# A mixture-of-experts stage in units of 120 rows, two units of an expert per task, task list made on the chip

## What is computed

```
x = x + tanh(g0) * attention(layernorm(x), context)      # one 32-wide head, tiled, @ Wout + bout
z = layernorm(x)
probs = softmax(z @ router_w.T)                          # 8 experts
weights, indices = top_k(probs, 2); weights /= sum + 1e-6
gate, up = split(z @ w13[e])                             # 512 -> 2 x 1024
y[e] = (silu(gate) * up) @ w2[e]                         # 1024 -> 512
x = x + tanh(g1) * sum over the two chosen e of weights * y[e]
```

## Time and profile before

| | |
|---|---|
| median of 3 runs | 400.83 us (398.74 to 402.16) |
| the profiled execution | 402.54 us |
| its span, first to last instruction | 400.9 us |
| PE busy | 375.2 us, 94% |
| PEld, DVE, ACT, POOL busy | 285.9, 221.8, 190.7, 143.1 us |
| HBM read | 70.95 MB |

### The profile page before, as it was taken

One profiled execution on the slowest core, in us unless ns is written; L12 is line 12 of the kernel. 1 busy time (PEld: TensorE's weight loads), 2 busy tenths in 40 slices (PEclk: granted clock), 3 DMA queues, 4 the chain that ended last, 5 costly groups with the idle time before them and its releaser, 6 DMA issues.

```text
span 400.9 us, 7148 instructions
## 1 busy us (share of the span) xinstructions
PE 375.2 (94%) x2034; PEld 285.9 (71%) x2035; DVE 221.8 (55%) x448; ACT 190.7 (48%) x313; POOL 143.1 (36%) x245
## 2 busy tenths in 40 slices
PE   3979799987999999999989999999999999999993
PEld 3335355565788888887868888888888888888882
DVE  3341767876934951899731249518932962694120
ACT  1123256656625832888621258328723842682220
POOL 2630768777333222514233242132303322331301
PEclk9977699999699999999999999999999999999997
DMA  7997689932169992499961239915952792200211
GB/s 251 361 366 262 239 294 356 266 134 69 17 246 398 368 327 45 138 346 352 356 203 30 27 52 336 314 35 138 337 214 53 260 329 91 46 26 7 34 18 17
DMA packets 18793, 77.79 MB, mean 194 GB/s; under 512 B 4827, under 2 KB 6075, under 8 KB 11612
## 3 DMA queue, kind: packets, MB, share of 16 engines
q1 hardware_dynamic: 11836, 66.82, 46.4%
q0 software_dynamic: 5184, 7.54, 9.9%
q10 hardware_dynamic: 1760, 3.28, 2.5%
HBM read 70.95 MB, written 7.58 MB: 196 GB/s over the span
## 4 chain that ended last, share of the span: by engine, by line
PE 61%; DMA 19%; POOL 6%; issue 6%; POOLq 2%; DVE 2%; ACT 1%; SPq 0%; DVEq 0%
PE scp L500 15%; PE turnB L480 14%; PE turnA L480 14%; DMA out_dram<-yw,ent 7%; DMA ent_next<-lists_d 7%; PE kvp L316 5%; PE kvp L487 2%; DMA xn<-in_x_dram 2%; PE turnA L369 2%; POOL ent_next L1123 1%; PE turnA L354 1%; PE scp L467 1%; DMA xg<-xn_d,ent_next 1%; PE scp L342 1%; DMA lists_d<-entry,place 1%
## 5 line engine op out<-in xcount | busy, mean ns | idle before, releaser
L847 DVE TENSOR_TENSOR w13l<-stage,w13h 128x1024 fp32r<-128x1024 f32 x64 | 75.9, 1218 | 4.7 <-ACT w13h L610 4.7
L610 ACT ACTIVATE w13h<-stage 128x1024 fp32r<-128x1024 f32 x64 | 65.0, 1053 | 0.0
L480 PE MATMUL turnA<-w13h,xTh 128*128 128x512 f32 x128 | 51.7, 404 | 2.1 <-DVE xTl L973 2.1
L480 PE MATMUL turnB<-w13h,xTh 128*128 128x512 f32 x128 | 51.9, 405 | 0.0
L480 PE MATMUL turnA<-w13l,xTh 128*128 128x512 f32 x128 | 51.4, 401 | 0.0
L480 PE MATMUL turnA<-w13h,xTl 128*128 128x512 f32 x128 | 51.4, 401 | 0.0
L500 PE MATMUL scp<-w2h,hTh 128*128 128x512 f32 x128 | 51.3, 401 | 0.0
L480 PE MATMUL turnB<-w13l,xTh 128*128 128x512 f32 x128 | 50.5, 395 | 0.0
L480 PE MATMUL turnB<-w13h,xTl 128*128 128x512 f32 x128 | 50.5, 394 | 0.0
L500 PE MATMUL scp<-w2h,hTl 128*128 128x512 f32 x128 | 50.1, 391 | 0.0
L500 PE MATMUL scp<-w2l,hTh 128*128 128x512 f32 x128 | 50.1, 391 | 0.0
(11 more groups left out here) (179 smaller groups left out, 632.0 us busy)
## 6 DMA issues: line engine op xcount, KB each, us to landing
stage<-in_w_dram SPq DMA_DIRECT2D x48, 1024.0 KB, 5.4
ctx_t<-in_ctx_dram SPq DMA_DIRECT2D x8, 1444.0 KB, 12.8
xT_t<-in_xT_dram SPq DMA_DIRECT2D x8, 200.0 KB, 12.1
xn<-in_x_dram SPq DMA_DIRECT2D x8, 200.0 KB
xn_d<-xn ACTq DMA_DIRECT2D x8, 200.0 KB
stage<-in_wout_dram SPq DMA_DIRECT2D x1, 1024.0 KB, 13.8
out_dram<-x ACTq DMA_DIRECT2D x4, 200.0 KB
out_dram<-yw ACTq DMA_DIRECT2D x2, 200.0 KB
```

The lines of the kernel that those rows point to most:

```text
L480: mm = pe.matmul(region, xp[:, c, :], wp[:, q, c, :], start=(c == 0 and i == 0), stop=(c == HC - 1 and i == 2))
L610: act.activation(dst, src, ACT.Copy).then_inc(S["w_hi"], 1)
L847: dve.tensor_tensor(lo, raw, hi.bitcast(F32), ALU.subtract).then_inc(S["w_lo"], 1)
```

## The change

- **Units.** Rows are handled in units of U = 120. List capacity per expert grows to 840 rows. A task is either a *single* (one unit) or a *pair* (two units of one expert, 240 rows).
- **Task list.** Task 0 is the first unit of expert 0. Then come the pairs of all experts, in order, then the odd units of all experts, in order. DVE and PE compute the row and the expert of each task (`task_row`, `task_e`) and the ends of the loops (`bounds`). The two matmuls for the table stand in task 0, behind its gate/up 0; the reads of the table by DVE give `tiles_ready`, for which POOL (first list read), SP (first load of the next weights) and the loops wait. Before, `tile_row` was made ahead of the first tile.
- **Weights.** They are loaded and split once per task, not per expert: every task, task 0 and the last included, splits the weights of the next one. For the last this is a load that nobody uses.
- **Single.** As a tile before, with 120 rows; x of both units of the next task is transposed (8 transposes, the second four into kvp). Its splits stand where they stood in a tile with splits.
- **Pair.** Gate/up holds a 128 x 128 block of w13 as the stationary operand and streams the 240 rows of x past it: 8 rounds of 24 matmuls. The result has h's features on partitions, so h is not transposed. Down is as before, once for each unit.
- **Task 0.** The low parts of units 4 to 9 of expert 0's weights are made between its products (`first_single`).
- **Rows.** Two gathers, two weight gathers and two scatters per task; xg_b and yw_b are second buffers.

```diff
+    U = 120
+    U2 = 2 * U
+    CAP = (-(-T // U) + 1) * U
...
-            sp.wait_ge(S["gathered"], 16)
-            with sp.Fori(1, E) as e:
+            sp.wait_ge(S["gathered"], 32)
+            sp.wait_ge(S["tiles_ready"], 1)
+            loads_end = sp.value_load(bounds[0:1, 2:3], min_val=2, max_val=TILES - 1)
+            with sp.Fori(1, loads_end) as t:
+                e = sp.value_load(task_e[0:1, bass.ds(t, 1)], min_val=0, max_val=E - 1)
                 for q in range(NQ):
-                    sp.wait_ge(S["w_lo"], e * W_UNITS - W_UNITS + 2 * q + 2)
+                    sp.wait_ge(S["w_lo"], t * W_UNITS - W_UNITS + 2 * q + 2)
...
+            def make_table():
+                pe.wait_ge(S["tabs_made"], 10)
+                pe.matmul(scp[0:1, 64:64 + TILES], ones[0:E, 0:1], tabs[:, 5, :], start=True, stop=True)
+                pe.matmul(scp[0:1, 128:128 + TILES], e_col[:], tabs[:, 6, :], start=True, stop=True).then_inc(S["table_done"], 1)
...
+            def single(t, aside=None):
+                gate_up(t, 0)
+                if aside is not None:
+                    aside()
+                gate_up(t, 1)
+                gate_up(t, 2)
                 turn_h(t, 0)
                 turn_h(t, 1)
-                gate_up(t, 3, e)
-                down(t, 0, e)
+                gate_up(t, 3)
+                down(t, 0)
                 turn_h(t, 2)
                 turn_h(t, 3)
-                turn_x(t + 1)
...
+                turn_x(t + 1, 0)
+                down(t, 1)
+                pe.wait_ge(S["hl_done"], 8 * t + 14)
+                turn_x(t + 1, 1)
+                down(t, 2)
+                down(t, 3)
+
+            def gate_up_pair(t, r):
+                if r == 0:
+                    pe.wait_ge(S["xl_done"], 2 * t + 2)
+                pe.wait_ge(S["h_done"], 8 * t + r + 5)
+                q, j = r // 2, r % 2
+                bank = (turnA, turnB)[r // 2 % 2][:, j * 512:(j + 1) * 512]
+                terms = ((w13h, xTh), (w13h, xTl), (w13l, xTh))
+                for part in range(2):
+                    cols = slice(part * QW + j * P, part * QW + (j + 1) * P)
+                    for c in range(HC):
...
+                        for i, (wp, xp) in enumerate(terms):
+                            mm = pe.matmul(bank[:, part * U2:(part + 1) * U2], wp[:, q, c, cols], xp[:, c, :],
+                                           start=(c == 0 and i == 0), stop=(c == HC - 1 and i == 2))
+                mm.then_inc(S["gu_done"], 1)
...
+            def pair(t):
+                for r in range(2 * NQ):
+                    gate_up_pair(t, r)
+                down_pair(t, 0)
+                turn_x(t + 1, 0)
+                turn_x(t + 1, 1)
+                pe.sem_inc(S["ht_done"], 2 * NQ)
+                down_pair(t, 1)
+
+            pe.sem_inc(S["xg_turned"], 2)
+            single(0, make_table)
+            pairs_end, tasks_end = task_ends(pe)
+            with pe.Fori(1, pairs_end) as t:
+                pair(t)
+            with pe.Fori(pairs_end, tasks_end) as t:
+                single(t)
...
+            def single(t):
 
                 def split(*units):
-                    if e_next is not None:
-                        for unit in units:
-                            split_hi(e_next, unit, t)
+                    for unit in units:
+                        split_hi(t + 1, unit, t)
 
                 silu(t, 0)
                 split(0, 1)
...
+            def pair(t):
+                for r in range(2 * NQ):
+                    silu_pair(t, r)
+                    if r > 0:
+                        h_hi_pair(t, r - 1)
+                    if 0 < r < 2 * NQ - 1:
+                        split_hi(t + 1, r - 1, t)
...
+            def first_single():
+                split_lo(0, 4)
+                split_lo(0, 5)
+                h_mul(0, 0)
+                split_lo(0, 6)
+                split_lo(0, 7)
+                h_mul(0, 1)
+                split_lo(0, 8)
+                h_mul(0, 2)
+                h_lo(0, 0)
+                h_lo(0, 1)
+                split_lo(0, 9)
+                h_mul(0, 3)
+                h_lo(0, 2)
+                h_lo(0, 3)
+                split_lo(1, 0)
+                x_lo(1)
+                for unit in range(1, W_UNITS):
+                    split_lo(1, unit)
...
+            make_tabs()
             make_weights()
+            read_table()
             dve.wait_ge(S["lists_sent"], 1)
-            for unit in range(4, W_UNITS):
-                split_lo(0, unit)
...
+            first_single()
...
-            with pool.Fori(1, n_tiles) as t:
+            with pool.Fori(1, tasks_end) as t:
                 entries_stay(t)
                 read_list(row_of(t + 1))
-                hold(S["xg_turned"], t + 1)
+                hold(S["xg_turned"], 2 * t + 2)
                 gather(t + 1)
                 gather_weights()
-                add_rows(t - 1)
+                add_rows(t)
                 entries_pass(t)
                 pool.drain()
```

More of the change, by code:

```diff
@@ L219, in unit_of, with task_ends @@
             return down[:, u * IC // 2:(u + 1) * IC // 2, :]
[L221 to L230, removed]
+        def task_ends(eng):
+            eng.wait_ge(S["tiles_ready"], 1)
+            return (eng.value_load(bounds[0:1, n:n + 1], min_val=2, max_val=TILES - 1) for n in range(2))
         @block.sync
@@ new lines, in down_pair @@
+            def down_pair(t, u):
+                if u == 0:
+                    pe.wait_ge(S["y_ready"], 2 * t + 2)
+                pe.wait_ge(S["w_lo"], t * W_UNITS + 2 * NQ + 1 + u)
+                terms = ((hTh, w2h), (hTl, w2h), (hTh, w2l))
+                for k in range(2):
+                    for j in range(u * IC // 2, (u + 1) * IC // 2):
+                        if k == 0:
+                            pe.wait_ge(S["hl_done"], 8 * t + j + 9)
+                        for i, (hp, wp) in enumerate(terms):
+                            mm = pe.matmul((scp, kvp)[k][0:U, 512:512 + H], hp[:, j, k * U:(k + 1) * U], wp[:, j, :],
+                                           start=(j == 0 and i == 0), stop=(j == IC - 1 and i == 2))
+                    if u == 1:
+                        mm.then_inc(S["y_done"], 1)
+                if u == 0:
+                    mm.then_inc(S["y_half"], 1)
@@ L603, in split_hi @@
                     if unit < 2 * NQ:
-                        act.wait_ge(S["gu_done"], NQ * last + NQ + unit // 2 + 1)
+                        act.wait_ge(S["gu_done"], 8 * last + 2 * (unit // 2) + 2)
                     elif unit == 2 * NQ:
@@ L665, in _, with h_hi_pair @@
+            def h_hi_pair(t, r):
+                act.wait_ge(S["h_done"], 8 * t + r + 9)
+                act.wait_ge(S["y_done"], 2 * t + 2)
+                act.activation(hTh[:, r, :], h_t[:, r % NQ, 0:U2], ACT.Copy).then_inc(S["hh_done"], 1)
             first_x_hi()
@@ new lines, in read_table @@
+            def read_table():
+                dve.wait_ge(S["table_done"], 1)
+                dve.tensor_scalar(task_row[:], scp[0:1, 64:64 + TILES], float(E * CAP), None, ALU.add).then_inc(S["rows_read"], 1)
+                dve.tensor_copy(task_e[:], scp[0:1, 128:128 + TILES]).then_inc(S["rows_read"], 1)
+                dve.wait_ge(S["rows_read"], 2)
+                dve.sem_inc(S["tiles_ready"], 1)
+            def x_lo(t):
+                for k in range(2):
+                    dve.wait_ge(S["xh_done"], 2 * t + k + 1)
+                    cols = slice(k * U, (k + 1) * U)
+                    dve.tensor_tensor(xTl[:, :, cols], (scp, kvp)[k][:, 0:HC * U].rearrange("p (c s) -> p c s", c=HC),
+                                      xTh[:, :, cols].bitcast(F32), ALU.subtract).then_inc(S["xl_done"], 1)
@@ L951, in split, with single @@
+            def single(t):
                 def split(*units):
-                    if e_next is not None:
-                        for unit in units:
-                            split_lo(e_next, unit)
+                    for unit in units:
+                        split_lo(t + 1, unit)
                 h_mul(t, 0)
@@ new lines, in pair @@
+            def pair(t):
+                for r in range(2 * NQ):
+                    h_mul_pair(t, r)
+                    if r > 0:
+                        h_lo_pair(t, r - 1)
+                    if 0 < r < 2 * NQ - 1:
+                        split_lo(t + 1, r - 1)
+                h_lo_pair(t, 2 * NQ - 1)
+                for unit in range(2 * NQ - 2, 2 * NQ):
+                    split_lo(t + 1, unit)
+                x_lo(t + 1)
+                for unit in range(2 * NQ, W_UNITS):
+                    split_lo(t + 1, unit)
@@ L985, in _ @@
-            t0, t1 = tiles_of(dve, E - 1)
-            with dve.Fori(t0, t1) as t:
-                tile(t, None)
+            first_single()
+            pairs_end, tasks_end = task_ends(dve)
+            with dve.Fori(1, pairs_end) as t:
+                pair(t)
+            with dve.Fori(pairs_end, tasks_end) as t:
```

(1 more changed line is left out.)

341 lines of the change are left out of this document (194 added, 147 removed).

## The result

The changed kernel takes 413.1 us (411.97 to 415.0, 4 runs), the one before, in the same session, 401.0: a ratio of 1.030. Some executions of a kernel are over 1.5% slower than its fastest one; the ratios with intervals in this document leave those out on both sides, so they differ a little from the ratio of the medians: here 1.037, with a 95% interval of 1.032 to 1.042. It is slower. Forecast were 412.0 us, 398 to 425, and a ratio of 1.028. The profiled execution, 413.6 us with a span of 412.0, ends where the sum of the prediction ended (412.1).

What follows compares the result with a forecast made beforehand. TensorE, busy 94% of the span, was taken to bound the kernel. Pair 1's start at 141.5, 0.4, six pairs of 34.5, three singles of 18.8, then 6.8 and 1.6 gave 413.7 us, on the median 412.0; range 398 to 425.

Steps and rivals of the forecast that it cites:

- Task 0: First single: silu 1 waits behind a load, TensorE stands for 16 us, pair 1 begins at 141.5, 20 us later.
- the splits ahead of the pair's first product: Start of pair 1: DVE works through eight units first, TensorE has four banks in hand; at most 0.5 us.
- The pair: Two units on TensorE: 34.5 us against 36.0 for two tiles; six pairs save 9 us.
- the 0.118 us of a 240-column matmul: Pairs' gate/up: 100 ns of columns plus 16 to 20 ns; 192 matmuls make 22.7 us.
- The singles: Last three tasks: each 18.4 us plus 0.4 for four more transposes, 18.8; three are 56.4 instead of 54.
- its lead of a pair covers that: Singles: POOL's lead covers 4.5 us of added gathers and scatters over three tasks; without it up to 10 us, none taken.
- The rival of the late POOL: POOL and DMA engines bound the singles: 22 instead of 18.8 us, up to 4 more in the stall, 420 to 425; chance 0.13.
- The dummy load: Load of task 10 at the end: lies behind task 9's y_out or beside the last scatter, costs nothing.
- Cheaper narrow matmuls: Pairs' gate/up: a matmul costs 0.100 us, a pair 31.1, the kernel 391; chance 0.10.
- Loads that are not hidden: Pairs' gate/up: operand load not hidden behind a narrow matmul, 0.211 us each, + 107 us, 519; chance 0.03.
- the F32 rate: Pairs' gate/up: narrow fp32r falls to F32's rate, 0.21 or 0.42 us per matmul, 520 or 760 us; chance 0.07.
- The pairs at the floor: Pairs' matmuls at 0.109 us, all else as summed: 402, no change; chance 0.12.

Runs made afterwards that it cites:

- The first experiment: Changed kernel with, in task 0 only, ACT making all silus, high parts and y_out before the ten splits of task 1's weights: 412.1 us, 1.049 of before.
- the lean POOL: Changed kernel with POOL gathering, scattering and keeping entries of only the first unit where the task is a single: 407.2 us, 1.026 of before.
- without the loads: Changed kernel with the singles at the end neither loading nor splitting weights: 407.6 us, a single run.
- the half-width run: Changed kernel with the second and third gate/up terms of the pairs streaming only 120 of the 240 rows: 411.4 us, a single run.
- the kernel that beats both: Changed kernel with table earlier, task 0 splits later, POOL setup moved, one-unit POOL in singles, remaining splits threaded through pair 1: 391.3 us, 0.973 of before.

## Why the prediction was right, and where its terms were not

- *Task 0.* The mechanism was the one forecast, link by link: table, list, gather, load, split, silu, product. 41.2 us were summed and 37.8 measured. Half of the difference is one link: the first gather took 1.1 us, not the 3.0 of the earlier trace rows; the text had named that case (2 less). The load was issued 18.4 us after the first matmul against 20.2 in the sum, and landed as assumed. The other half lies behind the hole: the clock was back at its upper level before gate/up 3 had ended (4.5 us instead of 5.1), and what stands behind down 0 took 5.4 us, not 6.1. The first experiment shows that ACT's order made this hole. That it alone can't be mended was not in the prediction: it counted the splits ahead of the pair's first product at 0.5 us at most, which is right with the hole and wrong without it.
- *The pair.* Forecast 34.5, measured 33.5. The term that was mis-sized is the 0.118 us of a 240-column matmul: it was built as columns plus the 16 to 20 ns that a 512-column one has besides, when the load, which the picks showed at 0.112, was the right row. 0.006 times 1152 matmuls is 6.9 us; a wait in pair 1 gave 0.9 back, where the sum had 0.4. The same floor is why the pair gains so little: 192 loads of 0.112 take nearly as long as 96 matmuls of 512 columns.
- *The singles.* Forecast 18.8 each and no cost for POOL, measured 20.3 on average and 1.4 us more after the last matmul. Without a wait a single is 18.4 (18.35 in the first), the four more transposes included. The step that failed is "its lead of a pair covers that". It covered the first single only. The rival of the late POOL, at 0.13, had the mechanism; it was a part of the result and not an alternative to it. The dummy load, priced at nothing, was not quite free: y_out of task 9 began at 404.8, 1.0 us behind the last matmul, after the split of the dummy's unit 8 (to 404.4) and POOL's entries (to 404.6). With the lean POOL the entries are early, and y_out still begins 0.5 us behind it; without the loads it is 0.1.
- *The start of the stage.* The sum had it begin 0.7 us earlier than before, and it began 2.1 later. The spread over the runs is larger than both.
- *The rivals.* Cheaper narrow matmuls: no, with the half-width run as proof. Loads that are not hidden, and the F32 rate: no, 0.112. The pairs at the floor: this is what happened, but it was priced as a change within 1%, with all the rest as summed; the singles took back what the pairs gave.
- *The signs.* Three of those named came as written: TensorE idle for 14.3 us, ended by h_t; the first load at 121.4; 66 loads of 1 MB, which are 11 units. Three did not: pairs 33.5 apart and not 34 to 35, starts 0.112 apart and not 0.116 to 0.120, singles from 18.4 to 21.7 and not 18 to 20.

With the start and POOL's part mended, the change pays. In the kernel that beats both, six pairs and three singles follow each other almost without a wait. Its six pairs take 203.3 us where 12 tiles took 218.3, 15.0 less (2.3 of it the late tile 5 and the like); task 0 takes back 4.0 of it, and the start, the singles and the end another 2.9, so that its span is 8.1 us shorter than that of before.

## What to carry to other kernels

Where a new first task is shorter than the one it replaces, ask what was prepared in the time that is gone, and follow that chain (table, list, gather, load) to the engine whose strict order it will block; one late input in front of a silu stopped every engine here. Moving the blocked instruction isn't enough: in two of the runs here the wait came back at the next place where the same order mattered. A wait of TensorE can cost more than its length: behind those of 5.1 and 7.0 us here the matmuls started at the lower clock, at nearly twice the distance. Before matmuls are made narrower, compare the columns with the load of the stationary operand: from 240 columns down to 120 next to nothing was saved (0.03 us in 5.4).

## What the runs showed of the hardware

- A matmul with a 128 x 128 fp32r operand to load starts 0.112 us after the one before on average, whether 240 or 120 columns stream; with 512 it is 0.229 to 0.233. At the granted clock's lower level (1.2 GHz) it is 0.213 with 240 columns and 0.43 with 512. The same slice used twice in a row is loaded twice.
- Indirect DMAs land later beside stage loads: a scatter under loads left POOL waiting up to 8.4 us for its landing (9.3 with the lean POOL), and without loads 1.5 to 3.3; the two gathers of task 1, next to loads issued early, made TensorE wait 3.9 us.
- The time at which the first stage ends varied by 5 us from one profiled execution to another, more than some of the effects that were looked for.
